# Group normalisation and two-head attention per image row: the cast of P before the residual sum, stores a row later, image loads of two rows

## The reference

```
x̂ = (x - mean) / sqrt(var + 1e-5)        # per image, over 32 groups of 4 channels, all rows and tokens
q, k, v = x̂ W_qkv^T + b_qkv              # 2 heads of 64 channels
score = softmax(q k^T / sqrt(128))       # within one row: 256 x 256 per head
out = x + score v                        # residual sum
```

## Time and profile before

| | |
|---|---|
| median of 3 runs | 4220.36 us |
| the profiled execution, its own time | 4225.53 us |
| its span | 4223.5 us, 147348 instructions |
| mean granted TensorE clock | 0.992 |
| busy: PE, DVE, ACT, POOL | 3958.7 (94%), 3759.4 (89%), 3125.2 (74%), 2134.7 (51%) |
| DMA engines, mean share | 0.9: queue of SP 79.7%, queue of ACT 10.7% |

### The profile page before, as it was taken

How to read it: one execution, slowest core, us unless ns; L and a number is a source line. 1 busy time by engine, 2 the same in 40 slices (tenths; PEclk the granted TensorE clock), 3 DMA queues, 4 the chain that set the end, 5 groups by cost and what they waited for, 6 DMA issues and landing times.

```text
span 4223.5 us, 147348 instructions
## 1 busy us (share of the span) xinstructions
PE 3958.7 (94%) x44133; PEld 2923.8 (69%) x44133; DVE 3759.4 (89%) x7138; ACT 3125.2 (74%) x8193; POOL 2134.7 (51%) x3089
## 2 busy tenths in 40 slices
PE   4999999899999999999999899999999999999998
PEld 3767777677776777767777677776767777677776
DVE  6998989889898898988989889898898989989887
ACT  3777777677776777767777677776777777777776
POOL 1555555455554555545555455554555555555554
PEclk9999999999999999999999999999999999999999
DMA  7999898998998989989899998989989998997878
GB/s 197 198 193 201 196 198 196 191 188 199 195 199 181 193 199 198 198 179 200 194 199 198 180 199 197 197 198 181 197 195 201 196 197 193 197 192 166 165 164 167
DMA packets 2438095, 809.81 MB, mean 192 GB/s; under 512 B 2175232, under 2 KB 2437760, under 8 KB 2437760
## 3 DMA queue, kind: packets, MB, share of 16 engines
q1 hardware_dynamic: 2311040, 679.97, 79.7%
q10 hardware_dynamic: 126720, 125.84, 10.7%
HBM read 134.42 MB, written 134.22 MB: 64 GB/s over the span
## 4 chain that ended last, share of the span: by engine, by line
issue 41%; POOL 26%; DVE 15%; POOLq 5%; PE 5%; DVEq 4%; ACT 2%; DMA 1%; SPq 0%; ACTq 0%
POOL p_hi L600 21%; DVE o_norm L455 9%; POOL x_ring L607 4%; POOLq L156 2%; DVEq L460 1%; PE o_bank L315 1%; DVE neg_max L429 1%; POOL y_ring L616 1%; ACT prob L394 1%; PE qk_bank L277 1%; DVE p_lo L436 1%; PE s_bank L299 1%; DVE v_lo L442 1%; POOLq L616 1%; POOLq L607 1%
## 5 line engine op out<-in xcount | busy, mean ns | idle before, releaser
L616 POOL TENSOR_TENSOR y_ring<-image,o_norm 128x256 f32<-128x256 f32 x1024 | 744.5, 727 | 2015.7 <-DVE o_norm L455 2009.9
L394 ACT ACTIVATE prob<-s_bank,neg_max 128x256 f32<-128x256 f32 x4096 | 1604.4, 481 | 189.8 <-issue 177.2
L375 ACT ACTIVATE qk<-qk_bank,b_in 128x256 f32<-128x256 f32 x2048 | 861.0, 472 | 757.2 <-PE qk_bank L277 755.6
L436 DVE SCALAR_TENSOR_TENSOR p_lo<-prob,p_hi 128x1024 f16<-128x1024 f32 x1024 | 1254.3, 1225 | 174.9 <-POOL p_hi L600 144.6
L429 DVE TENSOR_REDUCE neg_max<-s_bank 128x2 f32<-128x512 f32 x2048 | 1309.7, 681 | 35.8 <-PE s_bank L299 35.8
L299 PE MATMUL s_bank<-qk 64*128 64x256 f32 x8192 | 1172.1, 404 | 30.9 <-issue 30.0
L277 PE MATMUL qk_bank<-xc,w_norm 128*128 128x256 f32 x4096 | 1164.2, 407 | 0.0
L600 POOL TENSOR_SCALAR p_hi<-prob 128x1024 f16<-128x1024 f32 x1024 | 1071.4, 1046 | 22.8 <-ACT prob L394 18.1
L277 PEld LDWEIGHTS qk_bank<-xc,w_norm 128*128 128x128 f32 x4096 | 697.1, 190 | 394.9 <-issue 327.0
L299 PEld LDWEIGHTS s_bank<-qk 64*128 64x128 f32 x8192 | 709.4, 187 | 253.2 <-issue 205.3
L315 PE MATMUL o_bank<-v_hi,pt_lo 128*128 128x65 f16 x8192 | 852.9, 193 | 26.6 <-issue 18.0
(11 more groups left out here) (72 smaller groups left out, 2449.4 us busy)
## 6 DMA issues: line engine op xcount, KB each, us to landing
out_dram<-y_ring SPq DMA_DIRECT2D x512, 256.0 KB, 2.5
image<-in_x_dram ACTq DMA_DIRECT2D x240, 512.0 KB, 4.3
pt_hi<-p_hi SPq DMA_TRANSPOSE x1024, 3.3
pt_lo<-p_lo SPq DMA_TRANSPOSE x1024, 3.1
image<-in_x_dram SPq DMA_DIRECT2D x4, 2048.0 KB, 16.2
w_in<-in_L_conv_W_qkv_dram SPq DMA_DIRECT2D x1, 192.0 KB, 2.3
b_in<-in_L_conv_b_qkv_dram SPq DMA_DIRECT2D x3, 0.5 KB, 2.1
```

The costliest lines, as they stand in the source:

```text
L375: ins = act.activation(qk[:, v % 2, t, :], qk_bank[:, t * TOK:(t + 1) * TOK], ACT.Identity, bias=b_in[:, t:t + 1])
L394: ins = act.activation(prob[:, m, c:c + TOK], s_bank[m][h][:, a * TOK:(a + 1) * TOK], ACT.Exp, bias=neg_max[:, m, h, a:a + 1])
L436: dve.scalar_tensor_tensor(out=p_lo[:, v % 2, :], in0=prob[:, v % 2, :], scalar=P_SCALE, in1=p_hi[:, v % 2, :], op0=ALU.mult, op1=ALU.subt ...
L616: pool.tensor_tensor(y_ring[:, m, :], image[:, par, bass.ds(row, 1), :].rearrange("p a c -> p (a c)"), o_norm[:, v % 2, :, :].rearrange("p ...
```

## The change

Four edits. POOL's step is now cast, refill, sum, with the cast for row u instead of u-1 and the refill for row u+6 instead of u+5. DVE's step begins with the low half of P, and `v_low` stands ahead of `divide`. SP stores row u-7 instead of u-6. A load brings two rows instead of four and is issued in every second step.

```diff
-    CHUNKS = ROWS // UNROLL
+    LOAD_ROWS = 2
+    CHUNKS = ROWS // LOAD_ROWS
...
-                if coming is not None and u == 0 and bring is not None:
-                    bring(base, *coming)
+                if coming is not None and u % LOAD_ROWS == 0 and bring is not None:
+                    bring(base, u, *coming)
...
                 run(-2, transpose_low)
-                run(-6, store)
+                run(-7, store)
                 run(-1, transpose_high)
...
-                    act.wait_ge(y_done, base - (LAG - UNROLL))
-                rows = bass.ds(row, UNROLL)
+                    act.wait_ge(y_done, base + (u + LOAD_ROWS - LAG))
+                rows = bass.ds(row, LOAD_ROWS)
...
             def order(run, next_image):
+                run(-2, p_low)
                 run(-4, sums)
                 next_image(0)
-                run(-2, p_low)
+                run(-1, v_low)
                 next_image(1)
+                run(-4, divide)
                 next_image(2)
-                run(-4, divide)
-                run(-1, v_low)
                 run(0, row_max, 0)
...
             def order(run, next_image):
+                run(0, p_high)
+                run(+6, refill)
                 run(-4, finish)
-                run(+5, refill)
-                run(-1, p_high)
```

More of the change, by code:

```diff
@@ L190, in run_image @@
                         if bring is not None and i >= 0:
-                            for c in range(i, CHUNKS - LAG // UNROLL, start):
-                                bring(None, 1, 1, c * UNROLL)
+                            for c in range(i, CHUNKS - LAG // LOAD_ROWS, start):
+                                bring(None, 0, 1, 1, c * LOAD_ROWS)
                         step(i // UNROLL * UNROLL, i // UNROLL * UNROLL, i % UNROLL, par, None, None,
@@ L201, in run_image @@
                         step(t * UNROLL + g + start, t * UNROLL + start, u, par, None, None,
-                             None if last else (img + 1, 1 - par, t * UNROLL + (ROWS - LAG + start), first))
+                             None if last else (img + 1, 1 - par, t * UNROLL + (ROWS - LAG + start + u), first))
                 with eng.Fori(0, GROUPS // UNROLL) as t:
@@ L206, in run_image @@
                              None if last else (MEASURE, img + 1, t * UNROLL + u),
-                             None if final else (img + 2, par, t * UNROLL + (STATS_FROM - LAG)))
+                             None if final else (img + 2, par, t * UNROLL + (STATS_FROM - LAG + u)))
                 for i in range(FINISH):
@@ L411, in order, with bring @@
                 run(0, v_high)
-            def bring(base, img, par, row, free=False):
+            def bring(base, u, img, par, row, free=False):
                 if not (free or base is None or known_below(base, LAG)):
-                    act.wait_ge(y_done, base - (LAG - UNROLL))
-                rows = bass.ds(row, UNROLL)
+                    act.wait_ge(y_done, base + (u + LOAD_ROWS - LAG))
+                rows = bass.ds(row, LOAD_ROWS)
                 act.dma_start(image[:, par, rows, :], x_img[img, :, rows, :]).then_inc(loaded[par], 16)
```

## The result

The changed kernel takes **3974.27 us** (median of 4 runs, 3973.23 to 3977.71) against 4221.4 us for the kernel before in the same comparison: ratio 0.9416, 95% interval 0.9399 to 0.9432. The forecast was 4070 with a range of 3985 to 4175. It is close to the 3975 of the third rival ("all of it hidden").

What follows compares the result with a forecast made beforehand. A closed DVE-POOL ring of 3.94 us per row was taken as the bound; gains of 82 (measuring), 66 (plain) and 8 (statistics) less 5 (start) make 151, from 4225.5 to 4075, median 5 lower: 4070, range 3985 to 4175.

Steps and rivals of the forecast that it cites:

- third rival: All extras hidden: loads cost ScalarE nothing that matters, measuring rows 3.77 us and plain rows 3.66, total 3975; chance 12%.
- The ring through POOL: Closed wait loop: DVE's p_lo and o_norm, POOL's sum, refill and cast, then next p_lo; 3.94 us per row, the bound.
- TensorE's floor of 3.66: Plain rows, without image statistics work: TensorE's period 3.93 us less the 0.27 wait for v_lo, so at least 3.66 per row.
- The two-row ring that the loads lengthen: Plain rows: DVE, TensorE, ScalarE, POOL loop of 6.76 us per two rows; a 0.85 load gap makes 7.61, 3.81 per row.
- Measuring rows, DVE's own work: Rows that also measure the next image: DVE's work sums to 3.77 us; 3.82 taken against 3.99 before, gaining 82 us.
- the supplement: Extra above DVE's floor in measuring rows: 3.82 us per row taken where the floor was 3.77.
- Statistics rows: Last 12 rows per image, with small DVE statistics operations, some held by POOL: net 0.5 us gained per image, 8 in all.
- The store's place costs nothing: SP queue: storing a row later keeps the store from holding back the high half behind it; cost nothing.
- Smaller loads: Half-sized image loads move the same bytes and block a transpose for half as long; no gain was counted.
- Rival 1: POOL's cast takes the port before DVE's p_lo, which stands 1.04 us; at one row in four 4310 us; chance 12%.
- Rival 2: Another wait, transfers first of all, replaces the old bound in all rows: 3.92 us per row, 4170 to 4210; chance 16%.
- the 3.55 us that I took for a floor under everything: DMA engines busy 0.89 of each 3.99 us row, read as a minimum of 3.55 us per row.

## Why the prediction was right and where it failed

- **The ring through POOL bounded the kernel: right.** DVE's order alone made it 0.45 longer and rows became 4.39 us, as computed from the terms of the earlier trace rows. What went wrong are sizes: the profiled time was forecast as 4075 and came as 3973, and the terms for the plain, measuring and statistics rows below make 95 of these 102 us.
- **TensorE's floor of 3.66 in plain rows: right.** The earlier trace rows gave it, and the last image runs at 3.66 in the changed kernel, and at 3.65 to 3.67 in eight of the others; without the bias matmul, 0.12 us of TensorE's work, it runs at 3.56.
- **The two-row ring that the loads lengthen: this step failed**, the largest error, 0.10 x 364 = 36 us. The prediction took 3.78 where TensorE's own 3.66 to 3.68 came. Two terms were wrong. I let all of POOL's 2.08 us pass before p_lo; the rows after show that p_lo starts at 1579.89, right behind the cast that ends at 1579.86; it lets the refill pass (1.39 for 1.23), and the sum gives way (1.70). That takes the sum and most of the refill out of the ring, about 0.85 of its 6.76 us; even with a gap of 0.85 in it the ring is then 6.76 long (an estimate from these rows), or 3.38 per row, and binds nothing. And I charged 0.85 for the gap from the earlier trace rows; the issue itself is 0.39, and over all loads the gap before the exponentials had a median of 0.82 in the kernel before and has 0.48 now. One of the short ones:

```profile
1583.35 0.39 ACT L384 ACTIVATE v_hi<-v_bank 128x256 f16<-128x256 f32 x1
1583.48 0.39 ACTq L418 DMA_DIRECT2D image<-in_x_dram  x1
1583.98 1.57 ACT L395 ACTIVATE prob<-s_bank,neg_max 128x256 f32<-128x256 f32 x4 [0.25 <-issue]
```

  With loads of one row the ring should have closed in every turn, and nothing happened. The bound I had written down, 3.66, was the answer but for 0.02; I chose a value near the other end on a ring that I had not checked against the order in which the two engines take the port.
- **Measuring rows, DVE's own work: right in kind, 0.06 too long.** The floor came out as 3.72, not 3.77 (reciprocal 0.09 for 0.11, v_lo 0.31 for 0.34, o_norm 0.40, p_lo 1.13), and the supplement was 0.04: 480 x 0.06 = 29 us.
- **Statistics rows: 38 us gained, 8 forecast: this size failed too.** I had the holds right (0.69 to 1.00 for 0.15 to 0.42) but let two rows per image lose 0.6 to 1 each and the other ten win 0.1 to 0.3. There are four rows with four or five such operations, and they rose by only 0.2 to 0.4 (from 4.3 to 4.5 before to 4.6 to 4.9), since such an operation stands only for the rest of POOL's instruction; the other eight won 0.47 on average. The 30 us are the third part of the error.
- **The store's place costs nothing: right for the change.** The reason given, that the store must not hold back the high half behind it, is what the run shows. But I asked only whether the move harms and not what it saves. Left where it was the store would have cost 368 us, and the whole change would have been slower than the kernel before.
- **Smaller loads: 32 us**, priced at nothing. The prediction has the step that leads there (a smaller load holds a transpose for a shorter time) and gave it no value.
- **Rival 1**, a cast that takes the port ahead of p_lo: p_lo is 1.308 on average for 1.225, so it is held a little, at some places up to 1.80. But that is in the plain rows (mean 1.42), where DVE has room; in the 480 measuring rows, where DVE is the bound, the mean is 1.24 and 39 are over 1.30. Rival 2 did not come: the values' matmuls wait little, and 3.66 was reached. Rival 3 was the outcome, to within 1 us. That closeness is partly luck: plain rows stayed 0.02 over its floor, while measuring rows came 0.01 below theirs and the statistics rows gained 8 us more than it took; but 12% was too little for it, as both of its numbers were floors that I had read from rows.
- **The range** ended at 3985, above the 3975 that my own two floors gave. The extras that I put on the floors in plain and measuring rows turned out to be hidden for the most part, and the loss in the statistics rows was smaller than taken, so the three terms erred together and the same way.

## What to carry to other kernels

Look for a closed ring of hand-overs when rows with different amounts of work take the same time; lengthening it by a known amount is the cheapest proof. When one stage is moved ahead on an in-order engine, check every queue in which something waits for what now comes later, the store ahead of a transpose above all: one row of lead too many cost 393 us while the store stood at its old place (4342 against 3949), and 28 us after it was moved. Where a floor is read from rows and every extra above it is argued, put the forecast near the floor.

## What the runs showed of the hardware

- POOL and DVE exclude each other for a whole instruction when DVE's has two inputs in SBUF, in both directions: POOL's sum took 1.70 for 0.73 behind a p_lo, a DVE operation on 32 elements 0.69 to 0.72 for 0.18. TENSOR_SCALAR with one tensor input was held too (L520, w_norm, 1.00 for 0.40 to 0.42; its other operand is a column of scalars in SBUF). bn_stats, neg_max, v_lo and o_norm were not held.
- The DMA share is not a capacity: in the plain rows of the changed kernel it reads 1.07 at 3.68 us per row (columns as above), which is 3.94 us of packet time in a row of 3.68, so the 3.55 us that I took for a floor under everything was none.

```profile
1531.50:1605.10 73.60, 73.60 (x867) 58.41 (x867) 68.49 (x121) 59.85 (x162) 52.21 (x62) 1.00 1.07 218
```

- A load of 512 KB on ScalarE's queue delays a high-half transpose that SyncE issues while it is under way (landing 5.0 us for 3.3), enough to reach a cast of the next rows (214.7 us of such waits); one of 256 KB delays it less (3.9, and 52.7 us of waits).
- After TensorE had stood for 4.2 us where the outer loop jumps back, its granted clock was 0.50 (1.2 GHz) for 10.2 us in four places of the changed kernel and for 6.8 in one; without the bias matmul it was so for 3.4 to 6.8.

Open: what holds plain rows with loads at 3.63 once TensorE could do 3.56; and the stop where the outer loop jumps back, which no run here was made for.
